# Expert stage of a transformer block: each expert only on the rows that picked it

## What is computed

```python
def _swiglu(x, wg, wu, wd):
    return jax.nn.silu(x @ wg) * (x @ wu) @ wd
...
logits = xn @ gate_w.T
probs = jax.nn.softmax(logits, axis=-1)
tk_probs, tk_idx = jax.lax.top_k(probs, TOP_K)
tk_probs = tk_probs / (jnp.sum(tk_probs, axis=-1, keepdims=True) + EPS)
...
out = _swiglu(xf, sWg, sWu, sWd)
for e in range(NUM_EXPERTS):
    out = out + w[:, e:e + 1] * _swiglu(xf, Wg[e], Wu[e], Wd[e])
```

## Time and profile before

| | us |
|---|---|
| runs | 1051.43, 1053.46, 1058.31; median 1053.46 |
| span of the profiled execution, first to last instruction | 1048.5 |
| TensorE busy | 936.9 (89%) |
| VectorE busy | 728.0 (69%) |
| ScalarE busy | 519.4 (50%) |
| GpSimd busy | 371.1 (35%) |
| mean granted TensorE clock | 0.947 of full speed |
| DMA | 65.81 MB, 63 GB/s over the span |

### The profile page before, as it was taken

One profiled execution on the slowest core, in us unless ns is written; L12 is line 12 of the kernel. 1 busy time (PEld: TensorE's weight loads), 2 busy tenths in 40 slices (PEclk: granted clock), 3 DMA queues, 4 the chain that ended last, 5 costly groups with the idle time before them and its releaser, 6 DMA issues. The chain is left out here.

```text
span 1048.5 us, 19512 instructions
## 1 busy us (share of the span) xinstructions
PE 936.9 (89%) x5848; PEld 451.6 (43%) x5848; DVE 728.0 (69%) x2047; ACT 519.4 (50%) x954; POOL 371.1 (35%) x500
## 2 busy tenths in 40 slices
PE   6876899999999879999999879888889898989896
PEld 2331333333333323333333336656566555655564
DVE  6898777787778658777888546574757565666643
ACT  4551457777767546777777752323232323232321
POOL 4672122222222112222222415353535344454444
PEclk9895799999999979999999989999989999999999
DMA  6576652223333213322230203121213030403030
GB/s 159 155 160 150 167 83 45 39 41 60 58 56 60 43 22 56 59 44 39 43 59 5 44 26 85 49 63 45 67 35 77 11 101 7 104 3 89 5 87 10
DMA packets 112983, 65.81 MB, mean 63 GB/s; under 512 B 41198, under 2 KB 102159, under 8 KB 112655
## 3 DMA queue, kind: packets, MB, share of 16 engines
q1 hardware_dynamic: 108608, 62.73, 27.8%
q10 hardware_dynamic: 4274, 1.87, 0.7%
HBM read 51.21 MB, written 12.98 MB: 61 GB/s over the span
## 5 line engine op out<-in xcount | busy, mean ns | idle before, releaser
L254 DVE CUSTOM_DVE_ANT_0 x_in<-ps,mask 128x1024 bf16<-128x1024 f32 (+7 forms) x512 | 364.5, 755 | 87.7 <-PE ps L243 71.3
L905 ACT ACTIVATE expT<-ps 128x512 f32<-128x512 f32 (+1 forms) x640 | 330.6, 553 | 170.4 <-PE ps L1049 153.3
L1161 POOL TENSOR_TENSOR hu<-hu,q_space 128x512 f32<-128x512 f32 x128 | 169.7, 1327 | 214.7 <-DVE hu L1269 137.6
L1049 PE MATMUL ps<-q_space,kr 96*128 96x512 bf16 (+3 forms) x768 | 224.1, 338 | 14.7 <-ACT expT L905 8.4
L243 PE MATMUL ps<-kr,q_space 96*128 96x512 bf16 (+3 forms) x768 | 200.4, 347 | 19.8 <-DVE mx L254 11.5
L1269 DVE TENSOR_TENSOR hu<-gs,ps 128x512 f32<-128x512 f32 x144 | 98.6, 685 | 131.1 <-PE ps L1286 99.8
L1198 ACT ACTIVATE gs<-ps 128x512 f32<-128x512 f32 x144 | 86.1, 598 | 207.6 <-PE ps L1286 202.5
L1023 PE MATMUL ps<-expT,vr 128*9 128x256 f32 (+1 forms) x2560 | 180.7, 364 | 1.4 <-POOL expT L880 1.4
L880 POOL TENSOR_SCALAR_AFFINE_SELECT expT<-expT 128x512 f32<-128x512 f32 x128 | 82.3, 655 | 237.2 <-ACT expT L905 237.2
L1284 PE MATMUL ps<-xf_hi,w_hi 128*128 128x512 f32 x288 | 163.4, 567 | 0.0
L1297 PE MATMUL ps<-hu,wdn 128*128 128x512 f32 x288 | 154.5, 619 | 9.2 <-POOL hu L1161 9.0
(11 more groups left out here) (120 smaller groups left out, 716.9 us busy)
## 6 DMA issues: line engine op xcount, KB each, us to landing
q_space<-route SPq DMA_DIRECT2D x64, 256.0 KB, 5.6
q_space<-q_parts SPq DMA_DIRECT2D x48, 192.0 KB
kr<-k_parts SPq DMA_DIRECT2D x32, 128.0 KB
q_parts<-parts SPq DMA_DIRECT2D x24, 128.0 KB, 2.4
k_parts<-parts SPq DMA_DIRECT2D x24, 128.0 KB, 2.4
kr<-k_parts SPq DMA_DIRECT2D x16, 192.0 KB
x_in<-in_x SPq DMA_DIRECT2D x10, 256.0 KB, 3.1
v_ones<-v_st SPq DMA_DIRECT2D x8, 288.0 KB, 3.1
```

What stands on the lines that cost most here:

```text
L254: last = nc.vector.tensor_tensor_reduce(out=unread[:, odd, col:col + width], in0=psw[:, 2 * CT * odd + col:2 * CT * odd + col + width], in ...
L905: act.activation(expT[:, (NS * r + s) % PTN, hh, 0:width], ps[:, B_S + hh % 2, 0:width], ACT.Exp, scale=SCALE).then_inc(exp_ok, 1)
L1049: last = nc.tensor.matmul(ps[:, B_S + hh % 2, col:col + m], kr[:, r, hh, kt * P:(kt + 1) * P], qr[:, r, hh, q0:q0 + m], start=True, stop=True)
L1161: nc.gpsimd.tensor_tensor(hu[:, (2 * s + i + 2 * p) % 4], hu[:, (2 * s + i + 2 * p) % 4], w_all[:, p, s - 1], ALU.mult).then_inc(hw_ok, 1)
```

## The change

The whole of block three is replaced, and block two loses the preparation of chunk 0.

During attention, ScalarE fills an HBM buffer, sorted_rows, of 8 regions of 4096 rows and 1024 more, each row 130 float32 wide (the row, its weight, its number), with empty rows: eight DMAs, two at the end of each of groups 0 to 3. The weights lie expert by expert, gate and up side by side (512 columns); the down weights are loaded into w_gu, after the split, once attention is over.

Block three has three phases. The front phase prepares all 8 chunks in rounds n, with the shared expert of chunk n-2 in the same round, and routes pairs of chunks q: softmax, two picks, and a count by TensorE of how many rows before this one picked the same expert, which gives each pick its place in its expert's region. GpSimd then sends each row twice to its places, with 64 indirect DMAs of 128 rows. x_mid and the shared expert's result stay in the memory that q held. The tile phase takes 72 tiles of 128 rows, enough for 8192 picks with each expert's last tile partly empty, in 36 pairs q. A table made on one partition says where a tile starts (row_at, read into SyncE's registers) and which expert's weights it takes (w_at, read into TensorE's). Per pair: load, transpose, split, three passes per tile with the rows as the stationary operand and 512 weight columns moving, silu, product, four transposes, four down matmuls of 128 columns, scaling by the row's weight, and two indirect DMAs that write the rows to expert_rows by pick number. The sum phase loads both picks of every chunk, adds them to the shared result, normalizes, adds x_mid and stores.

```diff
+TOKENS = B * S
+PICKS = 2 * TOKENS
+REGION = TOKENS
+TILES = PICKS // P + NE
+SLOTS = NE * REGION + NE * P
+XW = P + 2
+COL_W, COL_ID = P, P + 1
+FILLS = 8
+FILL_TILES = SLOTS // P // FILLS
...
-        w_gu = sb(top, "w_gu", [P, 2, NE + 1, INTER])
-        wdn = sb(top, "wdn", [P, NE + 1, 2, P])
...
+        w_gu = sb(top, "w_gu", [P, NE + 1, 2 * INTER])
+        w_hi = sb(top, "w_hi", [P, NE + 1, 2 * INTER], F32R)
+        w_lo = sb(top, "w_lo", [P, NE + 1, 2 * INTER], F32R)
...
+                sp.wait_ge(lo_ok, 2)
+                for i in range(2):
+                    rows = slice(P * i, P * (i + 1))
+                    sp.dma_start(w_gu[:, 0:NE, rows], wd_d[:, rows, :].rearrange("e k h -> k e h")).then_inc(down_in, DMA)
+                    sp.dma_start(w_gu[:, NE, rows], swd_d[rows, :]).then_inc(down_in, DMA)
...
+                        if s == NS - 1 and isinstance(g, int) and g < FILLS // 2:
+                            act.wait_ge(empty_ok, 2)
+                            for i in range(2):
+                                lo = FILL_TILES * P * (2 * g + i)
+                                act.dma_start(xs_d[lo:lo + FILL_TILES * P].rearrange("(n p) w -> p n w", p=P),
+                                              empty[:].unsqueeze(1).to_broadcast([P, FILL_TILES, XW])).then_inc(filled, DMA)
...
+                for n in range(ROUNDS):
+                    if 2 <= n + 1 < CHUNKS:
+                        load(n + 1)
+                    if 1 <= n <= CHUNKS:
+                        c = n - 1
+                        sp.wait_ge(normed[1], c + 1)
+                        sp.dma_start(xs[:, c, 1, :, 0:E], xs[:, c, 0, :, 0:E]).then_inc(copied[c // 2 % 2], DMA)
+                regs = [sp.alloc_register(f"row{i}") for i in range(BATCH)]
+                sp.wait_ge(table, 10)
+                sp.wait_ge(sent, scattered(PAIRS))
+                for q in range(NP):
+                    if 2 * q % BATCH == 0:
+                        sp.load(regs, row_at[0:1, 2 * q:2 * q + BATCH])
+                    if q >= 4:
+                        sp.wait_ge(y_sent[q % 4], y_sent_until(q % 4, q - 4))
+                    for i in range(2):
+                        at = sp.snap(regs[(2 * q + i) % BATCH], min_val=0, max_val=SLOTS - P)
+                        sp.dma_start(xt[:, q % 4, i], xs_d[bass.ds(at, P), :]).then_inc(xt_in[q % 4], DMA)
+                for r in range(4):
+                    sp.wait_ge(y_sent[r], y_sent_until(r, NP - 4 + r))
+                for c in range(CHUNKS):
+                    wait(sp, z_ok, c - 2)
+                    for k in range(2):
+                        rows = slice(TOKENS * k + CT * c, TOKENS * k + CT * (c + 1))
+                        sp.dma_start(y_in[:, c % 3, k], y_d[rows].rearrange("(t p) e -> p t e", p=P)).then_inc(y_got[c % 3], DMA)
+                    if c >= 3:
+                        store(sp, c - 3)
+                for c in range(CHUNKS - 3, CHUNKS):
...
+                def scatter(q, k, ts):
+                    for t in ts:
+                        c = 2 * q + t // NT
+                        nc.gpsimd.indirect_dma_start(
+                            out=xs_d, out_offset=bass.IndirectOffsetOnAxis(ap=pos[:, q, k, t:t + 1], axis=0),
+                            in_=xs[:, c, k, t % NT], in_offset=None).then_inc(sent, DMA)
...
+                for n in range(ROUNDS + 3):
+                    q = (n - 5) // 2
+                    if n < CHUNKS:
+                        root(0, n)
+                    if n % 2 == 0 and n >= 6:
+                        q = (n - 6) // 2
+                        pool.wait_ge(rt, RT * q + RT)
+                        pool.wait_ge(ids_ok, 1)
+                        for p in range(2):
+                            pool.wait_ge(copied[q % 2], DMA * 2 * (q // 2 + 1))
+                        scatter(q, 0, range(0, PAIR_T))
+                    if n < CHUNKS:
+                        root(1, n)
+                        if n % 2:
+                            row_scale(n // 2)
+                    if n % 2 == 0 and n >= 6:
+                        scatter((n - 6) // 2, 1, range(0, PAIR_T))
+                for q in range(NP):
+                    r = q % 4
+                    pool.wait_ge(to_ok, q + 1)
+                    pool.wait_ge(y_kept, 2 * q + 2)
                     for i in range(2):
+                        nc.gpsimd.indirect_dma_start(
+                            out=y_d, out_offset=bass.IndirectOffsetOnAxis(ap=to[:, r, i:i + 1], axis=0),
+                            in_=yt[:, r, i], in_offset=None).then_inc(y_sent[r], DMA)
...
+                for c in range(CHUNKS + 1):
+                    if c < CHUNKS:
+                        pool.wait_ge(y_got[c % 3], DMA * 2 * (c // 3 + 1))
+                        nc.gpsimd.tensor_tensor(y_in[:, c % 3, 0], y_in[:, c % 3, 0], y_in[:, c % 3, 1], ALU.add).then_inc(y_sum, 1)
+                    if c > 0:
+                        root(2, c - 1)
...
+                def normalize(k, c, out, src):
+                    act.wait_ge(ln_ok[k], 4 * c + 4)
+                    for t in range(NT):
+                        last = act.activation(out[:, t], src[:, t], ACT.Identity, scale=rstd[:, k, c, t:t + 1],
+                                              bias=nb[:, k, c, t:t + 1])
+                    last.then_inc(normed[k], 1)
...
+                for n in range(ROUNDS + 1):
+                    b = n - LAG3
+                    if n < CHUNKS:
+                        keep_at(n)
+                    if 0 <= b < CHUNKS:
+                        keep_xf(b)
+                    if n % 2 == 0 and n >= 4:
+                        exps((n - 4) // 2)
+                    if 0 <= b < CHUNKS:
+                        silu(b, 0)
+                    if n < CHUNKS:
+                        act.wait_ge(ln_ok[0], 4 * n + 4)
+                        wait(act, mid_ok, n - 1)
+                        normalize(0, n, y1[:, n % 2], ps[:, B_PROJ].rearrange("p (t e) -> p t e", e=E))
+                    if 0 <= b < CHUNKS:
+                        silu(b, 1)
+                    if n < CHUNKS:
+                        normalize(1, n, xs[:, n, 0, :, 0:E], x_mid[:, n])
+                    if 0 <= b < CHUNKS:
+                        act.wait_ge(sh_down, b + 1)
+                        act.activation(shared[:, b].rearrange("p t e -> p (t e)"), ps[:, B_DOWN], ACT.Copy).then_inc(sh_kept, 1)
...
+                def keep_y(q):
+                    act.wait_ge(y_made, q + 1)
+                    if q >= 4:
+                        act.wait_ge(y_sent[q % 4], y_sent_until(q % 4, q - 4))
+                    for i in range(2):
+                        act.activation(yt[:, q % 4, i], ps[:, B_Y, P * i:P * (i + 1)], ACT.Copy,
...
+                keep_hi(0)
+                keep_hi(1)
+                for q in range(NP):
+                    tile_silu(q)
+                    if q + 2 < NP:
+                        keep_hi(q + 2)
+                    if q > 0:
+                        keep_y(q - 1)
+                keep_y(NP - 1)
...
+                for n in range(ROUNDS + 2):
+                    b = n - LAG3
+                    if n < CHUNKS:
+                        dve.wait_ge(projected, n + 1)
+                        stats(0, n, ps[:, B_PROJ].rearrange("p (t e) -> p t e", e=E))
+                    if 0 <= b < CHUNKS:
+                        dve.wait_ge(hi_ok, b + 1)
+                        v.tensor_tensor(x_lo[:, b % 2], xfT[:, b % 2], x_hi[:, b % 2], ALU.subtract).then_inc(lo_ok, 1)
+                    if n < CHUNKS:
+                        shift(0, n)
+                    for i in range(2):
+                        if 0 <= b < CHUNKS:
+                            dve.wait_ge(sh_up, 2 * b + i + 1)
+                            dve.wait_ge(sh_silu, 2 * b + i + 1)
+                            wait(dve, sh_down, b)
+                            v.tensor_tensor(hu[:, i], gs[:, i], ps[:, B_GU + 2 * i + 1], ALU.mult).then_inc(sh_hu, 1)
+                        if n % 2 == 0 and n >= 4:
+                            (route2_first, route2_second)[i]((n - 4) // 2)
+                        if i == 0 and n < CHUNKS:
+                            dve.wait_ge(normed[0], n + 1)
+                            dve.wait_ge(at_in[n % 2], DMA * AT_DMAS * (n // 2 + 1))
+                            v.tensor_tensor(x_mid[:, n], x1[:, n % 2], y1[:, n % 2], ALU.add).then_inc(mid_ok, 1)
+                            dve.wait_ge(mid_ok, n + 1)
+                            stats(1, n, x_mid[:, n])
+                    if n < CHUNKS:
+                        shift(1, n)
+                    if n % 2 and n >= 5:
+                        route3((n - 5) // 2)
+                    if n % 2 and 3 <= n < ROUNDS:
+                        route1((n - 3) // 2)
+                    if n % 2 and n < CHUNKS:
+                        row_var_of(n // 2)
...
+                def tile_h(q):
+                    b = 2 + 2 * (q % 2)
+                    dve.wait_ge(silu_ok, q + 1)
```

(83 more changed lines are left out.)

871 lines of the change are left out of this document (472 added, 399 removed).

## The result

The changed kernel took 1262.68 us (median of four runs, 1261.9 to 1266.18) against 1055.79 us for the kernel before: a ratio of 1.198, 95% interval 1.194 to 1.202. Its profiled execution took 1266.18 us, 1.9 us more than its span of 1264.3 us.

The account below looks back on a forecast made before the run. The prediction took TensorE arithmetic to bound the expert stage, six of eight products weighed with zero. Phase by phase, the first down product ended at 819, tiles at 1197, sums at 1236; 32 of fills and 5 gave 1273 us, range 1150 to 1430.

Parts of the forecast that it names:

- the loop that decides the tile phase: Tile phase: load(q+4) waits for pair q's landed scatter, so a pair takes 10.5 us although the input ring holds four.
- fills 32: Attention: each group's second fill holds ScalarE and TensorE can't catch up, four times 8 us, 32 us in all.
- 35 pairs and register loads: Tile phase: 35 pairs at 10.5 us, 368 us, plus 5 us for three sets of register loads.
- The preparation that left the last group: Attention's last group: chunk 0's preparation goes, 6 us less.
- The serial chain: Front phase: a chunk's whole chain makes one round without overlap, 12 us, or 13.5 with the shared expert, 17.5 with routing.
- the last 16: Scatter: the last 16 indirect DMAs come after all routing, at 1.3 us each, 21 us.
- The low end of a pair: Tile phase: scatters at 0.44 us, full clock and 0.55 us for keep_y give 7.1 us a pair.
- Cheap (1): Rival for scatters: 0.6 us each on GpSimd, landing in 1.3, a pair 8.8 us, about 1195 us; chance 0.18.
- dear (2): Rival for scatters: addresses cost 3 us a scatter, a pair 13.9 us, about 1445 us; chance 0.17.
- The third: Tile-phase rival: the ring doesn't bind, TensorE's 4 us a pair sets the pace, fills are free, 1013 us; chance 0.04.
- The fourth: Rival of near no change: a tile pair of 4.2 us with fills; chance 0.02.
- The Trainium skill's sum for a DMA issued by GpSimd: Tile phase: about 2.0 us fixed plus bytes over 436 GB/s, a pair 8.6 us, the whole 66 us less.

Follow-up runs that it names:

- e6: Changed kernel with fills apart, load waiting for the copy, turns behind down products and six sum-phase slots, plus next chunk's projection and first statistics a round earlier: 1016.29 us.
- e7: e6 with ranks and places worked out at the end of the even round and scatters between the roots in lots of four: 1002.08 us, ratio 0.954.
- e2: Changed kernel with the load of pair q+4 waiting for pair q's copy out of PSUM, not for its landed scatter: 1098.76 us, ratio 1.047.
- e3: Changed kernel with the transposes of pair q+2 put behind the down products of pair q-1, and ScalarE's copies likewise: 1165.61 us, ratio 1.113.
- e8: Changed kernel with each tile-phase scatter issued twice, the second into an unread array, and loads waiting for all four: 1349.84 us, ratio 1.287.
- e11: e4 with each tile-phase scatter issued twice, the second into an unread array: 1111.0 us, ratio 1.058.
- e4: Changed kernel with the edits of e2 and e3 together: 1070.97 us, ratio 1.021.
- e10: Changed kernel with the tile phase's scatters replaced by plain GpSimd DMAs, leaving out the placing of rows: 1209.57 us, ratio 1.152.
- e9: e7 with each group's second fill moved to its fifth step and all sum-phase loads issued ahead of all stores: 981.46 us, ratio 0.934.

## Why the prediction held

The time was right within about 10 us by luck: the terms cancel, though the loop that decides the tile phase was named rightly. The ledger, in us from the start of the span, the 32 us of fills put where they fall:

| step | predicted | measured | off |
|---|---|---|---|
| attention's end: 622.7 - 6 + fills 32 | 649 | 664.3 | +15 |
| start of stage three | 10 | 7.0 | -3 |
| rounds 0 to 11, to the last places | 157 | 165.1 | +8 |
| the last scatters | 21 | 33.6 | +13 |
| to the first down product's end | 14 | 16.5 | +3 |
| 35 pairs and register loads | 373 | 327 | -46 |
| landing of the last scatter | 5 | 5 | 0 |
| sum phase | 39 | 46 | +7 |
| span | 1268 | 1264.3 | -4 |
| from span to run | 5 | 1.9 | -3 |

**Fills.** The mechanism was right (a held second issue, TensorE idle under it), the size not. I took 25 ns a row with 150 rows queued and no hold for them. By the trace's packets of 520 B, a fill's 264 rows per engine took 13.4 to 14.9 us to move, 51 to 56 ns a row, and the second issue got through when 60 to 65 rows per engine of the first were left: half the credit at half the pace. That is four pauses of 13, not of 8. From the first to the eighth write to att the changed kernel took 174.8 us and the kernel before 118.2, 57 us more for a term of 32. Its first write came 3 us sooner and the step from its 15th to its 16th took 30.9 us instead of 35.7; no run shows why. The preparation that left the last group was worth 6.5 us, where I had put 6: from 570.9 us to the end the kernel before took 51.5 us, the same stretch of the changed kernel 45.0.

**Front rounds.** 12.4, 12.3, 14.2, 13.3, 17.2, 17.9 and 18.7 us for the first seven, against 12, 12 and a mean of 17 later. The serial chain is confirmed only in part: moving 4 us of each round ahead (e6) gave 13 of 32 us.

**Scatter.** 1.26 us each where I took 1.3. The term that failed is "the last 16": it was the last 32 that ran back to back, since ranks stood behind a round's down product and the third pair's places came late; with ranks moved (e7) the stretch behind the last places took 20.8 us, my 21, and the time fell by 14 us.

**Tile phase.** The loop was named before the run, and e2, e3, e8 and e11 bear it out from four sides. Its terms against the timeline: keep_y 0.7 (0.67), two scatters 2.6 (2.96, with 0.75 us from keep_y's end to the first issue), landing 1.6 (1.46 behind the second issue), issue and landing of the load 2.6 (2.42, since the second issue overlaps the landing), transposes 0.7 (0.48), down 1.9 (1.91). Together 9.90 for 10.5 with hand-overs. Over 32 pairs, the register loads included, it came to 9.87 us: 20 us less than my term, and the 5 us for register loads didn't show. The rest of the 46 us is in the count: the last three pairs wait for no load and took 11 us instead of 31. The low end of a pair, 7.1 us, adds up to 7.4 by its own terms. TensorE was busy for 53% of the phase, not under half, and the granted clock was 0.67, not near 0.5: in the middle of a pair, passes ran at 0.39 us again, and only the first ones after the pause and the down products at the lower level, 1.2 GHz.

**Rivals.** Cheap (1) and dear (2) scatters fell by 0.96 us an issue and a pitch of 1.26 us. The third, that the ring doesn't bind, is what e4 makes true: 3.9 us a pair, near its 4. It needs two edits, and the kernel as changed has neither. The fourth, near no change, took 4.2 us a pair with the fills as they are; e4 has 3.90 and came to a ratio of 1.021. The Trainium skill's sum for a DMA issued by GpSimd (DMA: Bandwidth & Descriptors, "Anatomy of one DMA"), 2.0 us plus bytes over its rate, gives 2.15 us for 64 KB, and the rows show 2.2 us from issue to landing. For one DMA the Trainium skill agrees with the rows. Two of them are not covered by its remark that making descriptors is a small part: here the second can't start until 1.26 us later, e10 shows 0.54 us for a plain one, and e8 that each is paid in full. A pair by the Trainium skill's sum was 8.6 us, measured 9.9.

**Sum phase.** Predicted 3.6 us a chunk; the adds came 4.3 apart. I had not seen SyncE's store in front of the next load (e9 against e7: 4.6 us) nor that root and statistics of neighbouring chunks alternate between GpSimd and VectorE.

## What to carry to other kernels

Before counting an engine's work, write out who frees a buffer slot and what is queued ahead of its next use: work of 3.9 us a pair ran at 9.9 us, and one wait and one swap of order brought it back, and with five smaller edits a change that cost 20% gains 6.6%. A slot is free when its last reader is done, not when the result made from it has landed. Look at each wait on the queue that issues loads, and keep large fills apart on an engine that computes: here the price was not in the bytes but in what stood behind the issue.
